# Scatters of edge records: batches of one in place of two, two batches in turn

## What is computed

```python
x = x + L0_gnn(layernorm(x), src, dst, edge_weight, w_self, w_neigh)   # gather x[src], weigh, sum by dst
x = x + L0_ffn(layernorm(x), ...)                                      # shared MLP + 2 of 4 experts
x = x + L1_gnn(layernorm(x), [src, dst], edge_attr_64, u, W1, b1, W2, b2)
x = x + L1_ffn(layernorm(x), ...)                                      # 2 of 8 experts

def L1_gnn(x, edge_index, edge_attr, ...):
    src = edge_index[0]
    sums = segment_sum(edge_attr, src, num_segments=n)                 # edges sorted by dst, summed by src
    counts = segment_sum(ones, src, num_segments=n)
    combined = concatenate([x, sums / maximum(counts, 1)[:, None], u[batch]], axis=1)
    return relu(combined @ W1 + b1) @ W2 + b2
```

## Time and profile before

| | us |
|---|---|
| median of 3 runs without the profiler | 3212.76 |
| lowest and highest of them | 3200.77 to 3222.05 |
| profiled execution, first to last instruction (its span) | 4237.5 |
| GpSimd busy in it | 1860.1 |
| TensorE busy in it | 2615.1 |
| VectorE, ScalarE busy in it | 1421.8, 974.8 |

### The profile page before, as it was taken

The page is one execution under the profiler, slowest core; times in us unless marked ns, Lnnn a source line. Parts: engine busy times, 40 slices in busy tenths (PEclk is TensorE's granted clock), DMA queues, the critical chain, the costliest instruction groups (busy, mean ns, idle before and its releaser), DMA issues. The chain is left out here.

```text
span 4237.5 us, 48325 instructions
## 1 busy us (share of the span) xinstructions
PE 2615.1 (62%) x11859; PEld 2002.8 (47%) x11860; DVE 1421.8 (34%) x3597; ACT 974.8 (23%) x2337; POOL 1860.1 (44%) x1901
## 2 busy tenths in 40 slices
PE   0445545556554221111211699998999879999998
PEld 0333334434443010100100466657996567888898
DVE  5211225666621000000000244438995542222222
ACT  4555222222220000000000244430003421111122
POOL 4566665665665777777777100002000342222222
PEclk9767667676776555555555799999998889999999
DMA  6223333332232111111111000006553454444455
GB/s 187 80 87 91 88 87 97 87 89 80 85 85 62 52 45 51 52 52 62 42 51 42 24 18 18 35 18 172 146 146 116 162 153 110 111 117 116 106 148 148
DMA packets 217917, 372.80 MB, mean 88 GB/s; under 512 B 48901, under 2 KB 146542, under 8 KB 216815
## 3 DMA queue, kind: packets, MB, share of 16 engines
q0 software_dynamic: 82928, 157.51, 14.4%
q1 hardware_dynamic: 77100, 154.03, 11.1%
q10 hardware_dynamic: 57812, 60.35, 5.0%
HBM read 290.03 MB, written 81.71 MB: 88 GB/s over the span
## 5 line engine op out<-in xcount | busy, mean ns | idle before, releaser
L673 PE MATMUL psum<-arena 128*128 x1984 | 632.1, 481 | 514.1 <-issue 325.7
L343 POOL DMA_INDIRECT arena<-xn_rows,arena x784 | 749.7, 956 | 449.7 <-issue 241.9
L904 POOL DMA_INDIRECT sorted_edges<-arena x768 | 766.7, 998 | 284.3 <-issue 265.1
L673 PEld LDWEIGHTS psum<-arena 128*128 128x128 f32 x1984 | 463.3, 243 | 683.1 <-issue 605.6
L408 ACT ACTIVATE arena<-arena 128x256 f32<-128x256 f32 x784 | 338.1, 496 | 697.3 <-DMA arena<-xn_rows,arena 642.6
L1177 PE MATMUL psum<-arena,acc 128*65 128x128 f32 x2720 | 311.9, 275 | 23.8 <-DVE arena L1330 23.8
L1177 PEld LDWEIGHTS psum<-arena,acc 128*65 128x65 f32 x2720 | 296.0, 138 | 40.1 <-DVE arena L1330 32.0
L1103 PE MATMUL psum<-arena 128*128 128x512 f32 (+1 forms) x336 | 172.3, 669 | 229.4 <-ACT arena L957 133.2
L1796 PE MATMUL psum<-arena,xr 128*128 x1344 | 301.7, 382 | 13.7 <-DVE xr L2021 9.1
L1783 PE MATMUL psum<-xr 128*128 128x256 f32 x1344 | 299.1, 381 | 1.0 <-DVE xr L2015 1.0
L575 DVE TENSOR_TENSOR acc<-acc,psum 128x256 f32 x248 | 103.0, 415 | 550.4 <-remote 366.8
(11 more groups left out here) (310 smaller groups left out, 3180.9 us busy)
## 6 DMA issues: line engine op xcount, KB each, us to landing
xr<-in_f_W_dram SPq DMA_DIRECT2D x63, 1024.0 KB
acc<-sorted_edges ACTq DMA_DIRECT2D x340, 132.0 KB, 2.2
arena<-in_attr_dram SPq DMA_DIRECT2D x28, 924.0 KB
arena<-xn_rows,arena POOLq DMA_INDIRECT x784
sorted_edges<-arena POOLq DMA_INDIRECT x784
arena<-hidden_parts SPq DMA_DIRECT2D x7, 1792.0 KB, 7.3
arena<-dispatched SPq DMA_DIRECT2D x42, 265.0 KB
arena<-in_f_W_dram SPq DMA_DIRECT2D x8, 1024.0 KB
```

The lines of the kernel that those rows point to most:

```text
L343: pool.indirect_dma_start(out=rows[:, c, :], out_offset=None, in_=xn_d, in_offset=bass.IndirectOffsetOnAxis(ap=idx[:, c:c + 1], axis=0)).t ...
L673: last = nc.tensor.matmul(psum[:, bank(u), 0:D], hot[:, u, c, :], rows[:, ds(slots[k] + c, 1), :].squeeze(1), start=c == 0, stop=c == RUN - 1)
L904: pool.indirect_dma_start(out=edges_d, out_offset=bass.IndirectOffsetOnAxis(ap=pos_i[:, c:c + 1], axis=0), in_=stage[:, q % 2, c % SC, :], ...
```

## The change

`EACH` goes from 2 to 1. With it `PER_TURN` goes from 14 to 28, and `SPENT` and `LANDED` are worked out anew from it. Every scatter from the third on now waits, on one of the two semaphores in turn, until the scatter two before it has landed: at most two are in flight. The instructions of every engine and their order are the same as before, but for the waits on GpSimd, which stand at every scatter in place of every second; what SyncE and ScalarE wait for is the same landings, counted by other numbers.

```diff
 SC = 28
 TURNS = 2
-EACH = 2
+EACH = 1
 PER_TURN = 2 * SC // (TURNS * EACH)
```

## The result

The changed kernel takes 3317.93 us (median of 4 runs), the one before 3214.3: 3.3% slower, ratio 1.0334, 95% interval 1.0299 to 1.037. The forecast was 3272 us within 3198 to 3350, slower. The direction came out as argued, and the change acts through the waits as argued; but the added time is 104 us where 60 were worked out, and 3318 lies above the forecast's own bounds, 3246 to 3307.

A forecast was written before the change was run, and what follows sets the result against it. The prediction took GpSimd's chain of scatters to set the end, so added time there is kernel time. To the median 3212.76 it added 33 (attribute loads), 12 (stores) and 15 (tile-sum loads), 60 us: 3272 us, range 3198 to 3350.

The forecast's parts named there:

- the round trip binds everywhere: Rival, chance 0.14: landing and wake-up take 2.75 us, so all scatter pairs slow, 78 us more, 3350 (3310 to 3390).
- the scatter that stops one earlier: Sign: after each load of attributes the first scatters stop at 28k+31 in place of 28k+32.
- the quiet step: Sign: scatter starts in quiet stretches stay 1.275 us apart; 1.3 or more would mean the round trip binds.
- What bounds the kernel: GpSimd's chain of gathers and scatters sets the end: 3246 us, against 3150 for the dense layers' chain.
- Hidden: Rival, chance 0.19: the dense chain, slowed by scatters, already ends last; GpSimd has slack and time stays 3213 (3190 to 3240).
- Faster: Rival, chance 0.08: fewer scatters in flight hold up the dense chain's loads and stores less: 3181 (3150 to 3190).
- Quiet stretches at no cost: Away from other transfers, landing and wake-up take 2.3 to 2.4 us against 2.55: cost 0, cover 0.15 to 0.25.
- Behind a load of attributes: A scatter held behind each of 26 loads costs one further step of 1.275 us: 33 us.
- The loads hold one scatter at most: Rival, chance 0.05: lateness after attribute loads is GpSimd's wake-up, so the 33 us go: 3240 (3225 to 3255).
- the rule on taking turns: DMA engines alternate queues by packet; a scatter would wait for a packet, not the whole load, and the 33 us go.
- Behind the stores: At 14 stores of hidden parts among the scatters, nothing to one step lost each: 0 to 18 us, 12 taken.
- Beside the loads of the tile sums: Some 187 scatters beside 264 loads each meet a queue of 0.3 us: 15 us taken, 0 to 43.

The follow-up runs named there:

- e4: The kernel before with batches of one and a single semaphore, so that each scatter waits for the one before it: 4222.58 us.
- e5: The kernel before with batches of one, eight in turn: 3136.22 us, ratio 0.9796.
- e8: The changed kernel with attribute loads of one column of 28, hidden-part stores of 64 KB into zeroed memory, and tile-sum loads held back until all scatters landed: 3486.77 us.
- e2: The changed kernel with its 26 loads of attributes bringing one column of 28: 3251.52 us.
- e3: The kernel before with its loads of attributes bringing one column of 28: 3160.59 us.
- e9: The kernel before with stores of hidden parts of 64 KB, the rest of that memory zeroed at the start: 3237.52 us.
- e0: The kernel before, run again without edit for a second recording: 3209.22 us.

## Why the prediction was right, and where its sizes were off

**The number: luck in part.** The measured 3318 isn't in the band of the forecast (3246 to 3307) but in that of *the round trip binds everywhere* (3310 to 3390). It is within the whole range of 3198 to 3350 because that takes in half of this rival's band. By the time alone one would have taken the rival for the cause; the step of 1.27 and e4 rule it out. Of the signs that were named, the scatter that stops one earlier and the quiet step came out; the scatters' stretch grew by 108 us where 33 were named.

**What bounds the kernel: right.** GpSimd's chain was put together from step times, since the first recording couldn't be taken as it stood. Its steps hold: second block's scatters from 1089.0 (1097 was worked out) to 2130.4 (2117). The sum overshot by 33 us since two errors are set against each other: the scatters end 13 us later than worked out, and from the last load of the tile sums (2201.1 in the second recording) to the end are 1006 us in place of 1057. The slack of the dense chain looks larger than the 96 us given: VectorE waits 178.5 us before the change, and still 110.8 in e5, where the time falls by 70 us with 66 us less of scatters. So *Hidden* and *Faster* had no ground here.

**Quiet stretches at no cost: right, by less than thought.** The cover is 0.08 us (e4). The rival *the round trip binds everywhere* was near, but didn't come.

**Behind a load of attributes: right mechanism, half the size.** 33 us were worked out as one step of 1.275 per load. By the timelines it is 2.57 - 1.75 = 0.82 a load. Over all 26 loads the first six starts of a quarter are together 2.62 us late in the median now and 1.61 before, 1.01 a load; 0.42 of it is the quarter's start, which is late with small loads too (e8). The rest is 0.59, or 15 us in all, as e2 and e3 have it (15.7). The step that was too large is that a whole step is lost: it took the hold to last equally long in both kernels. From the start of the scatter behind the load to that of the one waiting for it were 5.56 us before (1107.75 to 1113.31) and 4.68 now (1109.88 to 1114.56), so 0.88 of the step of 1.27 wasn't lost. *The loads hold one scatter at most* falls with e2: 55 us went, not under 15. As to the rule on taking turns in the Trainium skill ("DMA: Bandwidth & Descriptors", "Queues, rings and completion order"), the prediction took a packet to be much less than a load. The section has an engine drain a whole packet from one queue before it switches, and calls 9 to 17 descriptors typical of one. The load has 144 rows on queue 1 (first row below, the window from 1109.37 to 1114.4 of the changed kernel); spread evenly over 16 engines that is an estimated nine for each, so its whole share of an engine can be one packet. Read so, the rule leads to the hold that the traces show and not to *one scatter at most*; which rows make up a packet isn't seen in them. The load was issued at 1109.37, such loads land 4.7 us later in the median (second row), and the scatter that waited for the one behind the load starts at 1114.56, just after.

```profile
q1 hardware_dynamic: 144, 0.95, 59.5%
...
DMA to landing us min/median/max: 4.5/4.7/5.8
```

**Behind the stores: 12 us, measured 30.** A bound failed here: at most one step per store was taken over from the loads. But before the change a store was covered in full (e9), so the whole loss is new, 30 / 14 = 2.1 us a store, not a step's difference.

**Beside the loads of the tile sums: 15 us, measured 47**, above the upper bound of 43. The queue of 0.3 us for one load was right in kind and too small. An estimate says why: with a load every 0.92 us, as the prediction had it, 2.46 / 0.92 = 2.7 of them are issued in a round trip, not one. How many a scatter meets was not measured.

**Not in the sum: 43 us** that batches of one still lose against batches of two with these three made small or held back. The quarters' starts are 11 of them; late starts behind loads of instructions would be another 20 (22 against 1.5, inferred). The prediction had no term for either.

The loads came out too large and the other two too small; with what they share and the 43, the sum was 60 where 104 were measured.

## What to carry to other kernels

Where a queue is kept short by waits, subtract the measured round trip (2.46 us here) from the steps up to the transfer waited for (1.27 each): what is left, 0.08 us for two steps, 1.35 for three, 7.7 for eight, is the cover, and the holds behind other transfers are set against it. Here a cover of 0.08 us cost nothing in quiet stretches and 108 us beside other transfers. A profile that is a third longer than the runs could be used here by adding up its step times, to 1%; but record it again where that can be done.

## What the runs showed of the hardware

The step of an indirect scatter of 128 rows of 264 bytes is 1.27 us whatever its waits, as long as they are satisfied; the round trip with one in flight is 2.46. (Six starts, 112 scatters apart, come about 1.47 us late with two in turn and not with four or eight; why is open.) While most of a load of 924 KB ran (1108.5 to 1111.6 in e0), no packet of the three scatters issued by then did. One and the same kernel was recorded once with a span of 4237.5 us and once with 3207.5. Behind 16 of 18 loads of instructions in e8 a scatter came late, the one shown by 1.63 us; that the loads are the cause is inferred.
